# The order in which five engines take the stages of a fused macaron block, written out as explicit lists

## The chip, the cores and the metric

One core of a Trainium2 chip runs one program. The metric is the device time of that program in microseconds. The core has four compute engines, each with its own instruction stream: TensorE (PE in the profile), VectorE (DVE), ScalarE (ACT) and GpSimd (POOL); SyncE (SP) issues the DMAs. The streams run independently and meet only at semaphores.

## What is computed

The input x is 4 sequences of 1024 tokens with 128 features, all fp32. Three residual blocks follow each other:

```python
x = x + 0.5 * ffn(layernorm(x))
x = x + attn(layernorm(x))
x = x + 0.5 * ffn(layernorm(x))

def ffn(x):    # H = 512 hidden; m1, m2 are outer products of 16 tokens of the sequence
    h = x @ W1.T + scale * (x @ m1.T) + b1
    h = gelu(h, approximate=False)
    return h @ W2.T + scale * (h @ m2.T) + b2

def attn(x):   # 16 heads of 8; a linear attention over the whole sequence
    q, k, v = (split_heads(x @ W.T + b) for W, b in ((Wq, bq), (Wk, bk), (Wv, bv)))
    q, k = feature_map(q), feature_map(k)       # exp(x R - |x|^2 / 2), x over sqrt(8)
    kv = einsum('bhnd,bhne->bhde', k, v)
    z = 1 / (sum(q) + 1e-8)
    return merge(einsum('bhnd,bhde,bhn->bhne', q, kv, z)) @ Wo.T + bo
```

m1 and m2 depend on the sequence, so the FFN weights (W1 + scale m1) and (W2 + scale m2) are made anew for each sequence, in both FFN blocks.

## The kernel before

The 4096 tokens are cut into 8 chunks of 512, each held as 4 tiles of 128 tokens. A sequence is two chunks. FFN chunks are numbered 0 to 7 for the first FFN and 8 to 15 for the second, attention chunks 0 to 7. All activations stay in SBUF. Nothing is looped over on the chip: `build` writes each engine's stream, going through `plan(engine)`, a list of stages, and emitting for each one its waits and instructions.

A stage is written `name.chunk` or `name.chunk.part`, and may have halves on several engines. For an FFN chunk f:

- `stats.f`, `moments.f` (VectorE, L177, L189): mean and variance; `stats.f` on GpSimd (L196, L198): 1/sqrt by a power, giving `rstd`.
- `norm.f`: VectorE writes the normalised tiles `xn` (L546, four instructions); GpSimd then adds the bias to the whole chunk of X (L415).
- `turn.f`: TensorE transposes the four tiles into the bank `ps_t` (L690), ScalarE rounds to `xh` (L460), VectorE takes the rest `xl` (L565). The two halves of the number let the next matmuls keep precision.
- `up.f.j`, j = 0 to 3: three 512-wide matmuls (L718 to L720), then ScalarE's Gelu (L478). Two banks take turns, so `up.f.j` waits for the Gelu of two before it.
- `down.f.n`, n = 0 to 3: four fp32 matmuls, eight recorded instructions (L732); with n = 3, VectorE's residual add over the chunk (L614) and, for chunks 8 to 15, SyncE's store.

For a sequence i: `rows.i` writes 16 normalised tokens to DRAM and reads them back to every partition (`token_rows`, `ev`); `odd.i` (VectorE, L573) takes the other factor `od`; `w1.i` makes the weights of `up` on VectorE in twelve instructions, block by block (L590, L598, L602); `w2.i` makes those of `down` on GpSimd in two wide instructions, `w2m` and `w2e` (L425, L433). `up.2i.0` waits for the first block of `w1.i`, `down.2i.0` for `w2.i`. `od` and `ev` release both. `constants` and `split weights` prepare the attention weights once; `load` halves W2 on ScalarE.

For an attention chunk a: `astats`, `amoments`, `anorm`, `aturn` (as above, with the normalisation on ScalarE and GpSimd's add L419), `qk.a.n` (three matmuls, L749 to L751), `feat`, `head sums`, `exp` for the two halves of the chunk, `z sums`, `z eps`, `z` (VectorE, then GpSimd's product `qn`, L439), `qturn`, `gram`, per sequence `mix` in two parts, and `o.a` (TensorE L788, VectorE's add L659), after which the second FFN's `stats.(8+a)` may start. `turn.8` on TensorE waits for the add of `o.3`, since they share the bank `ps_t`.

The order of each engine's list comes from `TIMES`: for each engine, each of three phases and each stage, a time in steps of one chunk, for even and odd steps; `APART` overrides ten single stages. `plan` adds the step's number and sorts. No time of the table is waited for on the chip; it fixes only the order. Waits for buffers are in the stages themselves and do not depend on the order.

The lists that come out, in the stretches that the prediction speaks of (a blank in a name written as _):

```text
pool: stats.0 stats.1 norm.0 w2.0 stats.2 stats.3 norm.1 norm.2 w2.1
dve:  stats.0 moments.0 stats.1 moments.1 scale.0 norm.0 norm.1 odd.0 turn.0 w1.0 turn.1 stats.2 moments.2 stats.3 moments.3 norm.2 norm.3 odd.1 turn.2 constants.0 w1.1
pe:   warm_up.0.0 warm_up.0.1 turn.0 turn.1 up.0.0 up.0.1 up.0.2 up.0.3 up.1.0 up.1.1 down.0.0 up.1.2 up.1.3 turn.2 down.0.1 down.0.2 down.0.3 turn.3 down.1.0 down.1.1 split_weights.0 up.2.0
...
pool: stats.8 z.5 norm.8 anorm.7 stats.9 z.6 w2.4
dve:  o.2 feat.7.0 norm.8 z_sums.6 head_sums.7.1 o.3 z_eps.6 feat.7.1 z.6 mix.2.0 stats.9 odd.4 mix.2.1 turn.8 moments.9 w1.4 norm.9
pe:   o.3 turn.8 mix.2.0 gram.6 mix.2.1 qturn.5 o.4 gram.7 up.8.0 up.8.1 qturn.6 turn.9
...
pool: stats.15 w2.7 norm.15
dve:  norm.13 stats.14 down.10.3 turn.13 moments.14 norm.14 stats.15 odd.7 turn.14 moments.15 down.11.3 w1.7 norm.15
pe:   turn.14 up.13.2 up.13.3 down.12.2 down.12.3 down.13.0 down.13.1 up.14.0 up.14.1 turn.15
```

Of the kernel before, what the change touches and what calls it, by code (L numbers as in the profile page):

```python
# [27 lines left out]
SHIFT = 0.125  # L28
FC = 2 * CHUNKS

TIMES = {
    "sp": (
        {  # L40
# [21 lines left out]
        {
            "turn": (-0.62, -1.1), "up 0": (0.19, -0.18), "up 1": (0.33, -0.17), "load": (0.18, None),
            "up 2": (0.66, 0.39), "up 3": (0.81, 0.4), "split weights": (3.24, None), "anorm": (3.46, 3.85),
            "aturn": (4.84, 4.41),
        },
        {
            "feat 0": (0.34, 0.3), "feat 1": (0.96, 0.47), "exp 0": (1.35, 1.07), "exp 1": (1.42, 1.86),
            "gram": (None, 2.46), "qturn": (3.48, 4.43),
        },  # L70
        {
            "turn": (0.87, 0.49), "up 0": (1.44, 0.52), "up 1": (1.45, 0.53), "up 2": (1.5, 1.88),
            "up 3": (1.51, 1.89),
        },
    ),
    "dve": (
        {
            "stats": (-1.91, -2.53), "moments": (-1.9, -2.52), "norm": (-1.13, -2.1), "scale": (-1.14, None),
            "turn": (-0.39, -0.92), "odd": (-0.44, None), "w1": (-0.22, None), "constants": (1.62, None),
            "down 3": (2.12, 1.86), "astats": (2.49, 1.88), "amoments": (2.89, 3.11), "split weights": (3.57, None),  # L80
            "aturn": (4.91, 5.13),
        },
        {
            "head sums 0": (0.5, -0.02), "feat 0": (0.74, 0.67), "head sums 1": (0.95, 1.14),
            "feat 1": (0.97, 1.31), "z sums": (2.12, 1.92), "z eps": (2.28, 1.94), "z": (2.44, 1.96),
            "mix 0": (None, 3.51), "mix 1": (None, 3.93), "o": (4.99, 5.15),
        },
        {
            "stats": (-1.0, -0.48), "moments": (-0.97, -0.05), "norm": (-0.32, -0.02), "turn": (0.94, 0.02),
            "odd": (0.53, None), "w1": (0.97, None), "down 3": (3.01, 3.96),  # L90
        },
    ),
    "pe": (
        {
            "turn": (-0.89, -1.24), "warm up 0": (-1.13, None), "warm up 1": (-0.9, None), "up 0": (0.0, 0.0),
            "up 1": (0.14, 0.07), "up 2": (0.48, 0.09), "up 3": (0.55, 0.1), "down 0": (1.08, 0.8),
            "down 1": (1.12, 0.9), "down 2": (1.13, 1.29), "down 3": (1.66, 1.56), "split weights": (1.94, None),
            "aturn": (4.57, 4.14),
        },
        {  # L100
            "qk 0": (-0.22, 0.0), "qk 1": (-0.21, 0.01), "qk 2": (0.59, 0.16), "qk 3": (0.6, 0.17),
            "gram": (2.58, 2.15), "mix 0": (None, 2.8), "qturn": (3.18, 3.63), "mix 1": (None, 3.61),
            "o": (5.02, 4.23),
        },
        {
            "turn": (-0.63, 0.19), "up 0": (1.16, 0.25), "up 1": (1.17, 0.27), "up 2": (1.2, 0.81),
            "up 3": (1.22, 0.82), "down 0": (1.26, 1.64), "down 1": (1.28, 2.03), "down 2": (1.83, 2.21),
            "down 3": (2.62, 2.24),
        },
# [3 lines left out]
APART = {
    ("dve", "head sums", (2, 0)): 0.43,
    ("dve", "z sums", 7): 2.04,
    ("dve", "z eps", 1): 1.96,
    ("dve", "z eps", 7): 2.69,
    ("dve", "z", 1): 2.66,
    ("dve", "z", 7): 3.16,
    ("dve", "stats", 8): -2.28,  # L120
    ("dve", "moments", 8): -1.17,
    ("act", "anorm", 5): 3.35,
    ("act", "exp", (0, 0)): 0.76,
}


def work():

    for stage in ("load", "scale", "constants", "split weights"):
        yield stage, 0, 0, 0  # L130
    for k in range(2):
        yield "warm up", (0, k), 0, 0
    for f in range(FC):
        phase, step = (0, f) if f < CHUNKS else (2, f + CHUNKS)
        for stage in ("stats", "moments", "norm", "turn"):
            yield stage, f, phase, step
        if f % PER_B == 0:
            for stage in ("rows", "odd", "w1", "w2"):
                yield stage, f // PER_B, phase, step
        for j in range(HB):  # L140
            yield "up", (f, j), phase, step
        for n in range(NT):
            yield "down", (f, n), phase, step
    for a in range(CHUNKS):
        for stage in ("astats", "amoments", "anorm", "aturn"):
            yield stage, a, 0, a
        for n in range(NT):
            yield "qk", (a, n), 1, CHUNKS + a
        for p in range(2):
            yield "head sums", (a, p), 1, CHUNKS + a  # L150
            yield "feat", (a, p), 1, CHUNKS + a
            yield "exp", (a, p), 1, CHUNKS + a
        for stage in ("z sums", "z eps", "z", "gram", "qturn", "o"):
            yield stage, a, 1, CHUNKS + a
        if a % PER_B == PER_B - 1:
            for k in range(2):
                yield "mix", (a // PER_B, k), 1, CHUNKS + a
# [666 lines left out]
```

## Time and profile before

| | us |
|---|---|
| median of 3 runs | 191.21 |
| lowest, highest | 191.19, 191.68 |
| span of the profiled execution | 190.5 |
| TensorE busy | 172.3 |
| VectorE busy | 152.1 |
| ScalarE busy | 96.8 |
| GpSimd busy | 96.7 |
| mean granted TensorE clock | 0.981 |

The span runs from the first to the last instruction of one profiled execution. The page gives no other time for that execution; the median of the timed runs stands 0.7 us above its span. A busy TensorE is one with a matmul under way; two matmuls overlap a little, so their recorded lengths add up to more than the time they take. The chain of waits shows the time without the overlap. "issue" as a releaser means that the profile shows nothing that the engine waited for at that moment.

### The profile page before, as it was taken

Reading aid. Unit: us, or ns where it says so; the run is one execution under the profiler, and the core shown is the slowest. Engines: PE = TensorE matmul, PEld = TensorE weight load, DVE = VectorE, ACT = ScalarE, POOL = GpSimd, SP = SyncE. Lnnn points to the kernel's source line nnn. Section 1 sums busy time; section 2 is a strip of 40 time slices with the busy share of each in tenths; the row PEclk is TensorE's granted clock in tenths of the full one; section 3 lists DMA queues with packets and bytes.
Section 4 is the critical chain, followed back from the end, with each engine's and each line's share of the span. In section 5 each row is a group of like instructions: output and inputs, shape, how many; then the busy total and the mean of one; then the engine's idle time right before and its main releaser. Section 6 shows DMA issues by size and latency. Waiting matters only on the chain.

```text
span 190.5 us, 3499 instructions
## 1 busy us (share of the span) xinstructions
PE 172.3 (90%) x1115; PEld 150.9 (79%) x1115; DVE 152.1 (80%) x485; ACT 96.8 (51%) x170; POOL 96.7 (51%) x124
## 2 busy tenths in 40 slices
...
GB/s 139 222 135 252 109 6 0 3 109 3 5 110 5 0 0 0 3 2 0 0 3 0 0 2 112 0 3 44 69 0 58 112 57 55 34 137 23 87 3 110
DMA packets 17921, 9.60 MB, mean 50 GB/s; under 512 B 880, under 2 KB 17520, under 8 KB 17904
## 3 DMA queue, kind: packets, MB, share of 16 engines
...
q8 instruction: 9, 0.15, 0.3%
q14 instruction: 8, 0.07, 0.1%
...
## 4 chain that ended last, share of the span: by engine, by line
PE 55%; DVE 19%; issue 11%; DMA 7%; POOL 3%; ACT 2%; SPq 0%; DVEq 0%; POOLq 0%; ACTq 0%
PE quad L732 21%; PE quad L718 6%; DVE xn L546 6%; PE quad L720 5%; PE quad L719 5%; DMA ev<-token_rows 3%; PE ps_t L690 3%; PE quad L749 3%; DMA rows<-in_rows_dram 3%; PE quad L751 3%; PE quad L750 3%; DMA token_rows<-xn 1%; PE ps_g L767 1%; DVE ex L630 1%; DVE bst L177 1%
## 5 line engine op out<-in xcount | busy, mean ns | idle before, releaser
L478 ACT ACTIVATE gl<-quad,cols 128x512 f32<-128x512 f32 x64 | 43.5, 687 | 47.2 <-PE quad L720 46.4
L732 PEld LDWEIGHTS quad<-w2e,gl 128*128 128x128 f32 x496 | 60.8, 192 | 2.5
L732 PE MATMUL quad<-w2e,gl 128*128 128x128 f32 x496 | 62.0, 275 | 0.0
L546 DVE TENSOR_SCALAR xn<-X,mv,rstd 128x128 f32<-128x128 f32 x64 | 31.5, 555 | 6.2 <-POOL rstd L198 6.2
L718 PE MATMUL quad<-xh,w1h 128*128 128x512 f32 x64 | 29.4, 460 | 5.2 <-issue 4.0
L719 PE MATMUL quad<-xl,w1h 128*128 128x512 f32 x64 | 26.4, 413 | 0.0
L720 PE MATMUL quad<-xh,w1l 128*128 128x512 f32 x64 | 26.2, 410 | 0.0
L415 POOL TENSOR_TENSOR X<-X,b2h 128x512 f32<-128x512 f32 x16 | 20.4, 1281 | 8.7 <-DVE xn L546 8.7
L196 POOL TENSOR_SCALAR veps<-mv 128x4 f32<-128x4 f32 x16 | 4.3, 270 | 33.9 <-DVE mv L189 33.9
L614 DVE TENSOR_TENSOR X<-quad,X 128x512 f32<-128x512 f32 (+1 forms) x16 | 10.5, 658 | 13.6 <-PE quad L732 13.6
L718 PEld LDWEIGHTS quad<-xh,w1h 128*128 128x128 f32 x64 | 12.5, 196 | 8.9 <-issue 7.7
L460 ACT ACTIVATE xh<-ps_t 128x512 fp32r<-128x512 f32 x16 | 9.5, 592 | 19.2 <-PE ps_t L690 18.9
L198 POOL TENSOR_TENSOR rstd<-veps,mhalf 128x4 f32<-128x4 f32 x16 | 17.4, 1090 | 1.3
L690 PE MATMUL ps_t<-ident,xn 128*128 128x128 f32 x64 | 12.1, 289 | 5.6 <-DVE xn L546 2.9
L177 DVE BATCH_NORM_STATS2 bst<-X 128x6 f32<-128x128 f32 x64 | 13.7, 275 | 4.3 <-DMA X<-in_x_dram 4.3
L484 ACT ACTIVATE sq<-quad 128x512 f32<-128x512 f32 x16 | 9.5, 596 | 11.8 <-PE quad L751 11.6
L590 DVE SCALAR_TENSOR_TENSOR w1r<-ev,od,w1t 128x128 f32<-128x128 f32 x28 | 14.7, 544 | 1.0 <-issue 1.0
L690 PEld LDWEIGHTS ps_t<-ident,xn 128*128 128x128 f32 x64 | 7.8, 140 | 9.3 <-DVE xn L546 3.9
L720 PEld LDWEIGHTS quad<-xh,w1l 128*128 128x128 f32 x64 | 12.8, 200 | 3.0
L749 PE MATMUL quad<-wah,xah 128*128 128x512 f32 x32 | 13.9, 435 | 0.4 <-DVE ex L630 0.3
L468 ACT ACTIVATE xa<-X,anmr,arstd 128x128 f32<-128x128 f32 x32 | 13.1, 485 | 1.1 <-POOL anmr L409 1.1
L439 POOL TENSOR_TENSOR qn<-qk,zr 128x512 f32<-128x512 f32 x8 | 8.8, 1096 | 9.6 <-DVE zr L644 9.6
...
## 6 DMA issues: line engine op xcount, KB each, us to landing
ev<-token_rows SPq DMA_DIRECT2D x8, 512.0 KB, 3.8
...
```

The lines of the kernel that those rows point to most:

```text
L177: ins = dve.bn_stats(bst[:, i % 2, n], x[:, n])
L198: pool.tensor_tensor(rstd[:, i % 2], veps[:, i % 2], mhalf[:], ALU.pow).then_inc(s_rstd, 1)
L415: pool.tensor_tensor(X[:, xslot(i)], X[:, xslot(i)], b2h[:].unsqueeze(1).to_broadcast([P, NT, D]), ALU.add).then_inc(s_xb, 1)
L478: act.activation(gl[:, f % 2, j], ps_h[j % 2], ACT.Gelu, bias=cols[:, j:j + 1]).then_inc(s_gelu, 1)
L546: dve.tensor_scalar(xn[:, i % 2, n], X[:, xslot(i), n], mv[:, i % 2, n, 0:1], rstd[:, i % 2, n:n + 1], ALU.subtract, ALU.mult).then_inc(s_ ...
L590: dve.scalar_tensor_tensor(out=w1r[:, j], in0=even[:, j], scalar=od[:, j:j + 1], in1=w1t[:, j * D:(j + 1) * D], op0=ALU.mult, op1=ALU.add) ...
L690: ins = pe.transpose(ps_t[:, n * P:(n + 1) * P], xn[:, i % 2, n], ident[:])
L718: pe.matmul(ps_h[j % 2], w1h[:, w, blk], xh[:, f % 2], start=True, stop=False)
L719: pe.matmul(ps_h[j % 2], w1h[:, w, blk], xl[:, f % 2], start=False, stop=False)
L720: pe.matmul(ps_h[j % 2], w1l[:, w, blk], xh[:, f % 2], start=False, stop=True).then_inc(s_u, 1)
L732: ins = pe.matmul(y[:, n * P:(n + 1) * P], gl[:, f % 2, j, n * P:(n + 1) * P], w2e[:, f // PER_B % 2, j], start=(j == 0), stop=(j == HB - 1))
L749: pe.matmul(to, xah[:, a, tile], wah[:], start=True, stop=False)
```

## The change

`TIMES`, `APART` and `work` are removed. `ORDER` holds, for each engine, the list itself, and `plan` only splits it into words. Every stage of the lists before is in the lists after, once and on the same engine; the sequence differs on all five. What a stage emits, its waits, its buffers and its engine stay as they are. The new lists in full, with the removed tables cut:

```diff
@@ -28,145 +28,77 @@
 SHIFT = 0.125
 FC = 2 * CHUNKS
...
-TIMES = {
+ORDER = {
     "sp": (
-        {
-            "rows": (-0.84, None),
-        },
-        {
-        },
-        {
-            "rows": (-0.88, None), "down 3": (2.45, 2.43),
-        },
+        "rows.0 rows.1 rows.2 rows.3 rows.4 rows.5 rows.6 rows.7 down.8.3 down.9.3 down.10.3 down.11.3 down.12.3 "
+        "down.13.3 down.14.3 down.15.3 "
     ),
     "pool": (
-        {
-            "stats": (-2.74, -3.73), "norm": (-0.77, 0.15), "w2": (-0.75, None), "astats": (3.24, 2.28),
-            "anorm": (9.29, 8.79),
-        },
-        {
-            "z": (3.3, 2.34),
-        },
-        {
-            "stats": (-0.68, -1.2), "norm": (-0.65, 0.33), "w2": (1.31, None),
-        },
+        "stats.0 stats.1 stats.2 w2.0 norm.0 norm.1 stats.3 stats.4 w2.1 stats.5 stats.6 norm.2 w2.2 astats.0 stats.7 "
+        "astats.1 norm.3 norm.4 astats.2 norm.5 w2.3 astats.3 norm.6 norm.7 astats.4 astats.5 anorm.0 anorm.1 anorm.2 "
+        "astats.6 anorm.3 anorm.4 anorm.5 astats.7 z.0 z.1 z.2 z.3 z.4 anorm.6 stats.8 z.5 norm.8 stats.9 w2.4 "
+        "stats.10 stats.11 stats.12 z.6 w2.5 z.7 norm.9 norm.10 norm.11 stats.13 stats.14 anorm.7 w2.6 stats.15 "
+        "norm.12 norm.13 w2.7 norm.14 norm.15 "
     ),
     "act": (
...
+        "turn.0 up.0.0 load.0 turn.1 up.0.1 up.0.2 up.0.3 up.1.0 up.1.1 up.1.2 up.1.3 turn.2 turn.3 split_weights.0 "
+        "up.2.0 up.2.1 up.2.2 up.2.3 up.3.0 up.3.1 turn.4 up.3.2 up.3.3 turn.5 up.4.0 up.4.1 up.4.2 up.4.3 up.5.0 "
+        "anorm.0 turn.6 up.5.1 anorm.1 up.5.2 up.5.3 turn.7 up.6.0 up.6.1 up.6.2 aturn.0 anorm.2 aturn.1 up.6.3 "
+        "up.7.0 up.7.1 up.7.2 up.7.3 aturn.2 anorm.3 anorm.4 feat.0.0 anorm.5 exp.0.0 aturn.3 feat.0.1 feat.1.0 "
+        "aturn.4 exp.0.1 feat.1.1 feat.2.0 exp.1.0 exp.1.1 feat.2.1 anorm.6 feat.3.0 exp.2.0 exp.2.1 gram.1 aturn.5 "
+        "feat.3.1 anorm.7 aturn.6 exp.3.0 feat.4.0 exp.3.1 feat.4.1 aturn.7 qturn.0 feat.5.0 exp.4.0 exp.4.1 feat.5.1 "
+        "gram.3 qturn.1 feat.6.0 exp.5.0 exp.5.1 feat.6.1 qturn.2 qturn.3 feat.7.0 feat.7.1 exp.6.0 gram.5 exp.6.1 "
+        "exp.7.0 qturn.4 exp.7.1 turn.8 turn.9 qturn.5 up.8.0 up.8.1 gram.7 up.8.2 up.8.3 up.9.0 up.9.1 up.9.2 up.9.3 "
+        "turn.10 qturn.6 turn.11 up.10.0 up.10.1 turn.12 up.10.2 up.10.3 up.11.0 up.11.1 up.11.2 qturn.7 up.11.3 "
+        "up.12.0 up.12.1 turn.13 up.12.2 up.12.3 up.13.0 turn.14 up.13.1 up.13.2 up.13.3 up.14.0 up.14.1 turn.15 "
+        "up.14.2 up.14.3 up.15.0 up.15.1 up.15.2 up.15.3 "
     ),
     "dve": (
...
+        "stats.0 moments.0 stats.1 moments.1 scale.0 norm.0 odd.0 turn.0 norm.1 w1.0 stats.2 moments.2 turn.1 norm.2 "
+        "stats.3 stats.4 moments.3 constants.0 turn.2 moments.4 stats.5 down.0.3 odd.1 norm.3 norm.4 w1.1 astats.0 "
+        "turn.3 moments.5 stats.6 moments.6 turn.4 down.1.3 odd.2 norm.5 w1.2 norm.6 astats.1 amoments.0 down.2.3 "
+        "astats.2 stats.7 amoments.1 turn.5 moments.7 norm.7 turn.6 odd.3 w1.3 amoments.2 down.3.3 aturn.0 turn.7 "
+        "down.4.3 astats.3 astats.4 amoments.3 aturn.1 split_weights.0 down.5.3 amoments.4 astats.5 amoments.5 "
+        "down.6.3 aturn.2 astats.6 head_sums.0.0 amoments.6 feat.0.0 down.7.3 astats.7 aturn.3 head_sums.0.1 feat.0.1 "
+        "head_sums.1.0 feat.1.0 z_sums.0 amoments.7 head_sums.1.1 feat.1.1 head_sums.2.0 z_eps.0 feat.2.0 aturn.4 z.0 "
+        "head_sums.2.1 z_sums.1 feat.2.1 z_eps.1 head_sums.3.0 z.1 feat.3.0 aturn.5 z_sums.2 head_sums.3.1 z_eps.2 "
+        "feat.3.1 z.2 aturn.6 head_sums.4.0 z_sums.3 feat.4.0 head_sums.4.1 z_eps.3 aturn.7 feat.4.1 z.3 mix.0.0 "
+        "head_sums.5.0 mix.0.1 feat.5.0 z_sums.4 head_sums.5.1 z_eps.4 o.0 feat.5.1 stats.8 z.4 head_sums.6.0 mix.1.0 "
+        "moments.8 feat.6.0 o.1 z_sums.5 head_sums.6.1 mix.1.1 feat.6.1 z_eps.5 stats.9 z.5 norm.8 o.2 head_sums.7.0 "
+        "head_sums.7.1 moments.9 feat.7.0 o.3 feat.7.1 mix.2.0 norm.9 turn.8 odd.4 mix.2.1 w1.4 o.4 stats.10 turn.9 "
+        "o.5 moments.10 stats.11 stats.12 norm.10 moments.11 moments.12 z_sums.6 norm.11 z_eps.6 z.6 mix.3.0 z_sums.7 "
+        "stats.13 turn.10 odd.5 z_eps.7 w1.5 mix.3.1 moments.13 norm.12 turn.11 z.7 down.8.3 o.6 stats.14 moments.14 "
+        "down.9.3 odd.6 w1.6 turn.12 norm.13 norm.14 turn.13 o.7 down.10.3 stats.15 odd.7 moments.15 turn.14 w1.7 "
+        "norm.15 down.11.3 turn.15 down.12.3 down.13.3 down.14.3 down.15.3 "
     ),
     "pe": (
...
+        "warm_up.0.0 turn.0 warm_up.0.1 up.0.0 turn.1 up.0.1 up.0.2 up.0.3 up.1.0 up.1.1 up.1.2 turn.2 up.1.3 "
+        "down.0.0 down.0.1 down.0.2 down.0.3 down.1.0 split_weights.0 down.1.1 turn.3 down.1.2 down.1.3 up.2.0 up.2.1 "
+        "up.2.2 up.2.3 turn.4 up.3.0 up.3.1 down.2.0 up.3.2 down.2.1 up.3.3 down.2.2 down.2.3 turn.5 up.4.0 up.4.1 "
+        "down.3.0 up.4.2 down.3.1 down.3.2 up.4.3 down.3.3 up.5.0 turn.6 down.4.0 down.4.1 up.5.1 up.5.2 down.4.2 "
+        "down.4.3 up.5.3 turn.7 up.6.0 up.6.1 aturn.0 up.6.2 up.6.3 down.5.0 down.5.1 down.5.2 aturn.1 down.5.3 "
+        "up.7.0 up.7.1 aturn.2 up.7.2 up.7.3 down.6.0 down.6.1 qk.0.0 down.6.2 down.6.3 qk.0.1 down.7.0 down.7.1 "
+        "down.7.2 down.7.3 aturn.3 qk.0.2 qk.0.3 qk.1.0 qk.1.1 aturn.4 qk.1.2 qk.1.3 qk.2.0 qk.2.1 gram.0 qk.2.2 "
+        "qk.2.3 qk.3.0 qk.3.1 aturn.5 gram.1 qk.3.2 qk.3.3 gram.2 qk.4.0 aturn.6 qk.4.1 qturn.0 qk.4.2 qk.4.3 aturn.7 "
+        "gram.3 qk.5.0 qk.5.1 mix.0.0 qk.5.2 mix.0.1 qk.5.3 o.0 qk.6.0 qturn.1 qk.6.1 mix.1.0 qturn.2 qk.6.2 o.1 "
+        "qk.6.3 qk.7.0 mix.1.1 qk.7.1 qturn.3 o.2 qk.7.2 qk.7.3 gram.4 gram.5 o.3 qturn.4 mix.2.0 gram.6 turn.8 "
+        "mix.2.1 qturn.5 gram.7 turn.9 o.4 up.8.0 up.8.1 o.5 up.8.2 up.8.3 mix.3.0 up.9.0 up.9.1 down.8.0 up.9.2 "
+        "up.9.3 turn.10 down.8.1 down.8.2 down.8.3 down.9.0 mix.3.1 down.9.1 qturn.6 turn.11 up.10.0 up.10.1 down.9.2 "
+        "up.10.2 up.10.3 turn.12 o.6 down.9.3 up.11.0 up.11.1 qturn.7 up.11.2 up.11.3 down.10.0 down.10.1 down.10.2 "
+        "down.10.3 up.12.0 up.12.1 down.11.0 up.12.2 turn.13 down.11.1 down.11.2 o.7 down.11.3 up.12.3 up.13.0 "
+        "turn.14 up.13.1 up.13.2 down.12.0 down.12.1 down.12.2 down.12.3 up.13.3 up.14.0 turn.15 up.14.1 up.14.2 "
+        "down.13.0 down.13.1 down.13.2 up.14.3 down.13.3 up.15.0 up.15.1 down.14.0 up.15.2 up.15.3 down.14.1 "
+        "down.14.2 down.14.3 down.15.0 down.15.1 down.15.2 down.15.3 "
     ),
 }
...
 def plan(engine):
 
-    placed = []
-    for stage, i, phase, step in work():
-        name = f"{stage} {i[1]}" if isinstance(i, tuple) else stage
-        time = TIMES[engine][phase].get(name, (None, None))[step % 2]
-        if time is not None:
-            placed.append((step + APART.get((engine, stage, i), time), stage, i))
-    placed.sort(key=lambda p: p[0])
-    return [(stage, i) for _, stage, i in placed]
+    for word in ORDER[engine].split():
+        stage, *i = word.split(".")
+        i = tuple(int(k) for k in i)
+        yield stage.replace("_", " "), i if len(i) > 1 else i[0]
 
 
 def stats(dve, i, x, bst, s_bst, s_mv):
```

## Rows read from the trace of the kernel before

**Rows 1.** The page's busy table: us, share of the span, instructions.
```profile
PE 172.3 (90%) x1115; PEld 150.9 (79%) x1115; DVE 152.1 (80%) x485; ACT 96.8 (51%) x170; POOL 96.7 (51%) x124
```

**Rows 2.** Waits of TensorE: line, releaser, us in total, times, longest.
```profile
PE ps_t L690 <- DVE xn L546: 2.9, 4, 1.3
PE ps_r L672 <- DVE wb L525: 1.3, 1, 1.3
PE ps_m L706 <- DVE xal L576: 0.9, 1, 0.9
```

**Rows 3.** Windows: length; busy PE, PEld, DVE, ACT, POOL; granted clock; DMA.
```profile
10.00:15.00 5.00, 3.09 (x10) 2.24 (x11) 4.96 (x22) 1.80 (x3) 0.00 (x0) 0.76 0.59 174
78.00:114.00 36.00, 35.25 (x210) 29.63 (x208) 34.79 (x85) 24.15 (x50) 20.79 (x24) 1.00 0.00 1
120.00:125.00 5.00, 3.09 (x15) 1.96 (x15) 5.00 (x11) 2.14 (x4) 4.42 (x4) 1.00 0.00 0
125.00:130.00 5.00, 5.00 (x22) 4.35 (x23) 4.03 (x13) 2.13 (x4) 2.52 (x3) 0.66 0.01 3
```

**Rows 4.** The chain that ended last: start us, length us, what.
```profile
149.81 0.44 PE ps_t L690 x4
162.07 0.24 PE quad L718
162.77 0.89 PE quad L732 x8
```

**Rows 5.** Timeline: start, length in us, engine, line, operation, count, [wait before].
```profile
19.09 1.11 DVE L546 TENSOR_SCALAR xn<-X,mv,rstd 128x128 f32<-128x128 f32 x4 [1.88 <-POOL rstd L198]
19.35 1.04 POOL L198 TENSOR_TENSOR rstd<-veps,mhalf 128x4 f32<-128x4 f32 x1
20.36 2.52 POOL L415 TENSOR_TENSOR X<-X,b2h 128x512 f32<-128x512 f32 x2
20.42 3.05 DVE L546 TENSOR_SCALAR xn<-X,mv,rstd 128x128 f32<-128x128 f32 x4 [0.22 <-POOL rstd L198]
```

**Rows 6.** The timeline at 120 to 125 us.
```profile
120.70 1.21 POOL L439 TENSOR_TENSOR qn<-qk,zr 128x512 f32<-128x512 f32 x1
120.89 3.69 DVE L546 TENSOR_SCALAR xn<-X,mv,rstd 128x128 f32<-128x128 f32 x3
121.87 1.03 POOL L425 TENSOR_TENSOR w2m<-ev,od 128x512 f32<-128x512 f32 x1
122.98 1.52 POOL L433 TENSOR_TENSOR w2e<-w2m,w2t 128x512 f32<-128x512 f32 x1
```

**Rows 7.** Timeline of `w1.2` with `w2.2`, and of `w1.4` alone.
```profile
40.80 2.71 DVE L590 SCALAR_TENSOR_TENSOR w1r<-ev,od,w1t 128x128 f32<-128x128 f32 x2
41.83 1.53 POOL L433 TENSOR_TENSOR w2e<-w2m,w2t 128x512 f32<-128x512 f32 x1
44.35 0.47 PE L718 MATMUL quad<-xh,w1h 128*128 128x512 f32 x1 [0.97 <-issue]
...
118.52 0.57 DVE L590 SCALAR_TENSOR_TENSOR w1r<-ev,od,w1t 128x128 f32<-128x128 f32 x2
120.09 0.47 PE L718 MATMUL quad<-xh,w1h 128*128 128x512 f32 x1 [0.27 <-DVE w1l L602]
```

**Rows 8.** Timeline: TensorE's first instruction of `up.0.0` and of `up.2.0`.
```profile
12.56 0.69 PE L718 MATMUL quad<-xh,w1h 128*128 128x512 f32 x1 [0.68 <-DVE w1l L602]
...
29.24 0.47 PE L718 MATMUL quad<-xh,w1h 128*128 128x512 f32 x1
```

**Rows 9.** Timeline: `o.3` on VectorE, `up.12.0` and `up.14.0` on TensorE.
```profile
113.94 0.68 DVE L659 TENSOR_TENSOR X<-ps_t,X 128x512 f32<-128x512 f32 x1
...
156.41 0.47 PE L718 MATMUL quad<-xh,w1h 128*128 128x512 f32 x1 [1.19 <-issue]
...
172.20 0.47 PE L718 MATMUL quad<-xh,w1h 128*128 128x512 f32 x1 [1.54 <-issue]
```

**Rows 10.** DMA issues: count, KB each, median us from issue to landing.
```profile
ev<-token_rows SPq DMA_DIRECT2D x8, 512.0 KB, 3.8
```

88 lines of the change are left out of this document (removed).

## The prediction

> **What bounds the kernel now.** I read the busy table first: TensorE works 172.3 of 190.5 us, VectorE 152.1 [rows 1]. So the span is TensorE's work plus its stalls, and a new order can only change stalls. The waits of TensorE come next: it waits for VectorE's `xn` tiles, for `wb`, and for `w1l` [rows 2]. The windows show the third thing: from 78 to 114 us both engines are full (35.25 and 34.79 of 36 us), and twice the granted clock was low, at 10 to 15 us (0.76) and 125 to 130 us (0.66, so part of it at 1.2 instead of 2.4 GHz) [rows 3]. Last, the chain gives TensorE's step sizes: an `up` 0.70 us (162.07 to 162.77), a `down` 0.89, the four transposes of a chunk 0.44 [rows 4].
>
> The row that decides is one of VectorE beside GpSimd. A `norm` (four `xn` instructions) takes 1.11 us at 19.09, but 3.05 us at 20.42, where GpSimd runs two adds over a whole chunk (2.52 us) [rows 5]. At 120.89 it needs more than 3.69 us for three, beside `qn`, `w2m` and `w2e` [rows 6]: one `xn` gets through for each wide GpSimd instruction. The first block of `w1` is ready for TensorE 1.57 us after its start when GpSimd is quiet (118.52 to 120.09), and 3.55 us when `w2` lies beside it (40.80 to 44.35, with `w2e` ending at 43.36) [rows 7]. So what a new order is worth is which wide GpSimd work it puts beside which `norm` and `w1`. The diff adds no work; I followed it, adding these durations along the new lists.
>
> **Part 1, start to `up.2.0`.** Before, `up.0.0` starts at 12.56 and `up.2.0` at 29.24 [rows 8]. New: `norm.1` follows `turn.0` on VectorE, 1.1 us with GpSimd idle, so `w1.0` starts at 11.3 and `up.0.0` at about 12.8 (+0.2). `turn.1` now stands behind `up.0.0` on TensorE and behind `load.0` and a Gelu on ScalarE, so its VectorE half ends near 16.7. GpSimd has `stats.2` before `w2.0`: `rstd` is there at 16.3, and then `w2m`, `w2e` (1.03 and 1.53 us, [rows 6, 7]), `norm.0` and `norm.1` (1.26 us each, half of the 2.52 in [rows 5]) follow without a break until about 21.6. `norm.2` on VectorE starts at 16.65, right into these four, and ends near 21.8. TensorE's list has `turn.2` before `up.1.3` and before all of `down.0`, so it waits from 20.0 to 21.8, while `down.0` could have run from 19. VectorE goes on: `stats.3`, `stats.4`, `moments.3` (2.1), `constants` (about 2), `turn.2`, `moments.4`, `stats.5`, `down.0.3` to 28.3, then `odd.1`, which lets `w2.1` start beside `norm.3`: 31.6. `norm.4` 32.7, first block of `w1.1` 34.1. TensorE is idle from 29.3 to 31.6 before `turn.3` and 0.5 us before `up.2.0`. At 34.1 it has done two `down` more than before at 29.24 (1.8 us), so it is behind by 34.1 - 29.24 - 1.8 = 3.1 us. By idle time alone it is +2.4 (4.7 against 2.3) and +0.2 for the later start. I take 2.6.
>
> **Part 2, `up.2.0` to 80 us.** Of the old stalls (0.97 before `up.4.0` [rows 7], 0.9 for `xal` [rows 2], 0.3 before `up.6.0`) those for `xal` and `up.6.0` go: `aturn` now comes later. But ScalarE's `turn.4` stands behind `up.3.1`, so `norm.5` starts only at 42.1, again beside GpSimd's `norm.2` and `w2.2`, and TensorE loses 0.8 at `turn.5` and 1.2 at `up.4.0`. 2.0 against 2.3: -0.3. So at 80 us the new kernel is 2.3 us late.
>
> **Part 3, the full stretch.** The mark is the end of `o.3` on VectorE: 113.94 + 0.68 = 114.62 before [rows 9]. VectorE has no slack here, so what stands ahead of `o.3` in its list counts. Newly ahead: `aturn.4` 0.66, `stats.9` 0.85, `moments.9` 0.36; no longer: `z_sums.6` 0.65. That is +1.2. `norm.8` now stands right behind `z.5`, so GpSimd's `qn` (1.1 to 1.2 us, as in [rows 6]) lies on it: +1.0, of which I give back 0.6 for small VectorE gaps that close. Mark: 114.62 + 2.3 + 1.2 + 0.4 = 118.5.
>
> **Part 4, the mark to the end.** Before, 190.5 - 114.6 = 75.9 us. Three things get better. `norm.9` comes before `odd.4`, so `w2.4` can't lie beside it: 1.1 us instead of over 3.69 [rows 6], and TensorE has `turn.9` behind it early. `norm.12` and `norm.14` run long before `w1.6` and `w1.7` need their `ev` (its transfer takes 3.8 us [rows 10]), so the waits of 1.2 and 1.54 us before `up.12.0` and `up.14.0` [rows 9] go. Two get worse: `w1.4` and `w1.5` now lie beside `w2.4` and `w2.5`, 2 us each on the first block; and GpSimd's `norm.12` and `norm.13`, put behind `stats.15`, meet `w1.7` together with `w2.7`, which moves `norm.15` to 8 to 11 us behind TensorE's `turn.14`, where only 6.8 us of work cover it. Followed the stretch is 73.3 us with the last bunch at its lightest and 76.2 at its heaviest. I take 74.3, as the earlier steps of this part all gain.
>
> **The sum.** 118.5 + 74.3 = 192.8 us of span against 190.5. The median of the runs is 191.21, 0.7 above the span; so 193.5. Sizes I can't see: how much `xn` gets through before GpSimd takes over (+/-0.3 each time, some ten times), and a further low clock. Before, it was low after TensorE's waits ahead of `up.0.0` (the last 0.68 us [rows 8]), and again at 125 us after five microseconds in which TensorE worked 3.09 [rows 3]. New waits of 2.4 us before `up.8.0` can do the same; the old one is dropped with `turn.9`, so I count them even; at worst one more costs 1.7 us (three steps of 1.3 instead of 0.7).
>
> The Trainium skill, "SBUF — State Buffer", section "Who interferes with whom", says that the loser of the port shared by VectorE and GpSimd is blocked for the whole of the other's instruction. The rows on wide operands agree. By its letter the narrow GpSimd instructions would block too; but the trace has the narrow power (1.04 us at 19.35) beside `norm.2` (1.11 us for four, as fast as alone) [rows 5]. So they cost nothing in my sum; by the rule they would cost up to 1.04 us at `norm.7` (beside `astats.1`) and at `norm.11` (beside `stats.12`), 2 us in all, and the estimate would be 195.6.
>
> **Rivals.** (a) *Slower, as summed*: 192.3 to 194.9, chance 0.45. (b) *Faster*: the bunches are lighter than I have them. The one mechanism: `norm.2` gets most of its four `xn` through before `w2m` locks, and so `norm.3` and `norm.5`. Then `turn.2` is there at 18, TensorE loses nothing in part 1 and 2 (0 to +0.3), the mark is at 115.5, and with 73.3 to 74 behind it the span is 188.8 to 189.5: 189.5 to 190.3 measured. For it: VectorE's totals are the same and part 4 loses real waits; against it: the one-by-one pattern in [rows 5, 6]. It decides where `norm.2` ends before 19.5. Chance 0.30. (c) *No change*, 190.6 to 191.8: part 1 is late by 2 but VectorE's slack after 60 us swallows it before the mark. Against it: TensorE is full from 61 to 80 us in both. 0.10. (d) *Clearly slower*, 195 to 197: the heaviest bunch at `w1.7` (76.2) and one more stretch at 1.2 GHz: 118.5 + 76.2 + 1.7 + 0.7 = 197.1. 0.13, and 0.02 more for blocked narrow instructions. That the change does nothing is excluded: the lists have the same 219, 195, 142, 64 and 16 entries, but the order differs on every engine.
>
> **Numbers.** A measurement tells 0.3%, 0.57 us, from no change. Faster is (b), 0.31 with a little of (c); the same 0.09; slower 0.60. The range takes in most of (b) and of (d): 189.3 to 196.5.
>
> **What would show it.** `norm.2` on VectorE over 4 us long and an idle TensorE before `turn.2`, `turn.3`; `up.2.0` at 33 to 35 us; the end of `o.3` at 117 to 119; `up.12.0` without a wait; `norm.15` later than 8 us behind `turn.14`. It is wrong if `norm.2` takes less than 3 us, or if `up.2.0` starts before 32.

## The result: 193.6 us against 191.2, and a profile that does not show it

| | before | after |
|---|---|---|
| median of the first runs, us | 191.20 (4 runs) | 193.58 (4 runs) |
| lowest, highest | 191.18, 191.68 | 191.95, 194.15 |
| span of the profiled execution | 190.5 | 190.2 |
| its mean granted clock | 0.981 | 0.982 |

The ratio is 1.013, with a 95% interval of 1.0071 to 1.0189. Twelve more runs of the changed kernel (first experiment) gave 193.36, ratio 1.0071 (1.0034 to 1.0108). So the change costs 0.7 to 1.3% by the two estimates, a small loss but one clear of both intervals. Medians are of all executions; the ratios leave out those that took over 1.5% more than the fastest of the same kernel.

The two profiled executions differ by 0.3 us, the wrong way round. The profiled one of after was the fastest of its four: an execution's time is its span and 1.7 us, so 191.95 is 190.2, and the median of 193.4 over all sixteen executions is a span near 191.65. The spans of the other three were 191.3, 192.4 and 192.4, at granted clocks of 0.973, 0.965 and 0.965. What the change costs has to be looked for in the clock as well as in the trace.

The page after, busy table, answers to [rows 1]:

```profile
PE 170.8 (90%) x1115; PEld 149.5 (79%) x1115; DVE 149.2 (78%) x485; ACT 96.1 (51%) x170; POOL 96.3 (51%) x124
```

VectorE is busy 2.9 us less with the same 485 instructions: fewer of them are held up by GpSimd. Yet TensorE's waits for `xn` and `w1l` are longer than before (line, releaser, us in total, times, longest; L622, L650 and L478 are the L690, L718 and L546 of before, since the tables above them are shorter):

```profile
PE ps_t L622 <- DVE xn L478: 7.1, 5, 3.7
PE quad L650 <- DVE w1l L534: 4.4, 2, 2.3
PE quad L650 <- issue: 2.7, 3, 1.6
```

[rows 2] has the 2.9 us for `xn` of before; two further lines of the same view of before are needed beside it:

```profile
PE quad L718 <- issue: 4.0, 4, 1.5
PE quad L718 <- DVE w1l L602: 0.9, 2, 0.7
```

2.9 us for `xn` have become 7.1, one of these waits 3.7 us long, and 0.9 us for `w1l` have become 4.4. Against that, the waits under "issue" fell from 4.0 to 2.7, and those for `wb` and `xal` are gone. On balance TensorE is without a matmul for 19.4 us (190.2 less 170.8) instead of 18.2 (190.5 less 172.3): little is lost in sum, but more of it in single long waits. The windows say where, and what follows; they answer to [rows 3] (length, busy PE, PEld, DVE, ACT, POOL, clock, DMA, GB/s):

```profile
78.00:114.00 36.00, 35.67 (x213) 30.04 (x212) 35.20 (x83) 24.40 (x50) 18.07 (x22) 1.00 0.02 6
120.00:125.00 5.00, 2.82 (x15) 2.24 (x16) 5.00 (x18) 2.94 (x5) 1.03 (x1) 1.00 0.00 0
165.00:170.00 5.00, 1.33 (x7) 0.83 (x5) 5.00 (x8) 1.38 (x2) 4.13 (x4) 0.95 0.00 0
170.00:175.00 5.00, 5.00 (x27) 4.32 (x27) 2.27 (x5) 1.80 (x3) 1.28 (x1) 0.70 0.19 52
```

From 165 to 170 us TensorE works 1.33 of 5 us, while VectorE is full and GpSimd nearly so. Then the granted clock is 0.70: part of the next window runs at 1.2 GHz. Before, that happened at 125 to 130 us [rows 3].

The stretch in the middle of it, on VectorE (start, length, engine, line, operation, tiles):

```profile
162.78 1.36 DVE L522 SCALAR_TENSOR_TENSOR w1r<-ev,od,w1t 128x128 f32<-128x128 f32 x1
164.06 1.30 DVE L530 CAST w1h<-w1r 128x128 fp32r<-128x128 f32 x1
165.28 1.14 DVE L534 TENSOR_TENSOR w1l<-w1r,w1h 128x128 fp32r<-128x128 f32 x1
166.48 2.87 DVE L534 TENSOR_TENSOR w1l<-w1r,w1h 128x128 fp32r<-128x128 f32 x2
169.28 1.10 DVE L478 TENSOR_SCALAR xn<-X,mv,rstd 128x128 f32<-128x128 f32 x4
```

on GpSimd at the same time:

```profile
162.51 2.77 POOL L347 TENSOR_TENSOR X<-X,b2h 128x512 f32<-128x512 f32 x2
165.23 1.04 POOL L357 TENSOR_TENSOR w2m<-ev,od 128x512 f32<-128x512 f32 x1
166.35 1.58 POOL L365 TENSOR_TENSOR w2e<-w2m,w2t 128x512 f32<-128x512 f32 x1
167.90 1.31 POOL L347 TENSOR_TENSOR X<-X,b2h 128x512 f32<-128x512 f32 x1
```

and on TensorE:

```profile
169.76 1.15 PE L622 MATMUL ps_t<-ident,xn 128*128 128x128 f32 x4 [3.67 <-DVE xn L478]
```

Five wide GpSimd instructions in a row (162.5 to 169.2 us), and beside each about one of VectorE's twelve gets through. `w1.7` lasts 7.8 us, from 161.5 to 169.35, where a `w1` with GpSimd quiet takes 2.5 (experiment 6). `norm.15` stands behind it, `turn.15` behind that.

### The profile page after: what moved, and what is told of

It is laid out like the page before. It is cut to its first block, busy times and chain, and to the rows that moved or that the text cites. A ratio compares the mean times of both kernels' runs of the same rounds, so it can differ in the third digit from the quotient of the medians.

```text
span 190.2 us, 3499 instructions
## 1 busy us (share of the span) xinstructions
PE 170.8 (90%) x1115; PEld 149.5 (79%) x1115; DVE 149.2 (78%) x485; ACT 96.1 (51%) x170; POOL 96.3 (51%) x124
## 4 chain that ended last, share of the span: by engine, by line
PE 63%; DVE 21%; issue 8%; ACT 3%; DMA 3%; SPq 0%; DVEq 0%
PE quad L664 23%; DVE xn L478 8%; PE quad L650 7%; PE quad L651 6%; PE quad L652 6%; PE quad L681 3%; PE ps_t L622 3%; DVE w1r L522 3%; PE quad L683 3%; PE quad L682 3%; DMA rows<-in_rows_dram 3%; PE ps_g L699 2%; DVE w1l L534 2%; PE ps_m L638 2%; DVE bst L109 1%
## 5 line engine op out<-in xcount | busy, mean ns | idle before, releaser
L664 PEld LDWEIGHTS quad<-w2e,gl 128*128 128x128 f32 x496 | 59.5, 192 | 2.0
L664 PE MATMUL quad<-w2e,gl 128*128 128x128 f32 x496 | 60.2, 275 | 0.0
L650 PE MATMUL quad<-xh,w1h 128*128 128x512 f32 x64 | 29.3, 458 | 7.6 <-DVE w1l L534 4.4
L478 DVE TENSOR_SCALAR xn<-X,mv,rstd 128x128 f32<-128x128 f32 x64 | 29.4, 523 | 2.3 <-POOL rstd L130 2.3
L650 PEld LDWEIGHTS quad<-xh,w1h 128*128 128x128 f32 x64 | 12.7, 198 | 12.3 <-issue 10.5
L128 POOL TENSOR_SCALAR veps<-mv 128x4 f32<-128x4 f32 x16 | 4.5, 282 | 34.1 <-DVE mv L121 34.0
L546 DVE TENSOR_TENSOR X<-quad,X 128x512 f32<-128x512 f32 (+1 forms) x16 | 10.5, 658 | 11.6 <-PE quad L664 11.6
L622 PE MATMUL ps_t<-ident,xn 128*128 128x128 f32 x64 | 12.1, 301 | 7.2 <-DVE xn L478 7.1
L130 POOL TENSOR_TENSOR rstd<-veps,mhalf 128x4 f32<-128x4 f32 x16 | 16.9, 1053 | 1.3
L622 PEld LDWEIGHTS ps_t<-ident,xn 128*128 128x128 f32 x64 | 8.5, 148 | 10.9 <-issue 4.5
L497 DVE TENSOR_TENSOR xl<-ps_t,xh 128x512 fp32r<-128x512 f32 x16 | 10.9, 680 | 7.5 <-ACT xh L392 7.5
L522 DVE SCALAR_TENSOR_TENSOR w1r<-ev,od,w1t 128x128 f32<-128x128 f32 x28 | 15.4, 571 | 0.5 <-DVE od L505 0.5
L681 PE MATMUL quad<-wah,xah 128*128 128x512 f32 x32 | 14.4, 450 | 0.3 <-DVE ex L562 0.3
```

The lines of the kernel that those rows point to most:

```text
L130: pool.tensor_tensor(rstd[:, i % 2], veps[:, i % 2], mhalf[:], ALU.pow).then_inc(s_rstd, 1)
L478: dve.tensor_scalar(xn[:, i % 2, n], X[:, xslot(i), n], mv[:, i % 2, n, 0:1], rstd[:, i % 2, n:n + 1], ALU.subtract, ALU.mult).then_inc(s_ ...
L522: dve.scalar_tensor_tensor(out=w1r[:, j], in0=even[:, j], scalar=od[:, j:j + 1], in1=w1t[:, j * D:(j + 1) * D], op0=ALU.mult, op1=ALU.add) ...
L622: ins = pe.transpose(ps_t[:, n * P:(n + 1) * P], xn[:, i % 2, n], ident[:])
L650: pe.matmul(ps_h[j % 2], w1h[:, w, blk], xh[:, f % 2], start=True, stop=False)
L664: ins = pe.matmul(y[:, n * P:(n + 1) * P], gl[:, f % 2, j, n * P:(n + 1) * P], w2e[:, f // PER_B % 2, j], start=(j == 0), stop=(j == HB - 1))
```

## Experiments

Each had 6 to 12 runs, beside 11 to 35 of the kernel before in the same job. Times are medians. "The changed kernel" without a number stands for the 193.36 us of the first experiment. Experiments 1 to 4, 5 to 8, and 9 and 10 ran together, with medians of the kernel before of 191.83, 191.80 and 191.39 us.

**1. The changed kernel once more.** No edit.

> The changed kernel as it is, for more executions beside the kernel before. Its four times so far lie between 191.95 and 194.15 us, with granted clocks from 0.982 down to 0.965. Clock theory: the time follows the granted clock, in steps of about 1.1 us for each further stretch at 1.2 GHz, and no execution is under 191.9. Wait theory (the prediction's sum): the time is lost in waits that are there in every execution, so the spread is chance and not tied to the clock. Both expect a median of 193 to 194.

Measured: 193.36 us, 191.83 to 195.18. With a clock for every execution, the spans sort like this (the kernel before from all jobs, the changed kernel from both of its):

| mean granted clock | before: executions, median span | after: executions, median span |
|---|---|---|
| 0.989 to 1.0 | 46, 189.8 | 0 |
| 0.981 to 0.982 | 16, 190.15 | 5, 190.5 |
| 0.973 | 7, 191.7 | 8, 191.5 |
| 0.965 | 0 | 3, 192.4 |

At the same clock the two orders take the same time, within 0.35 us in the medians. These are small groups with a wide spread: the five of the new order at 0.982 lie between 190.1 and 192.0 us, so the mean clock does not fix the time. What differs clearly is how often they get which clock: two thirds of the old order's executions run at 0.989 or better, none of the sixteen of the new one. The medians of the clock groups lie 1.0 and 0.9 us apart, near the 1.1 of the clock theory; the fastest execution, 191.83, is just under its 191.9. The windows of the profiled execution of this run, beside those above:

```profile
165.00:170.00 5.00, 1.38 (x6) 0.77 (x5) 5.00 (x7) 1.38 (x2) 4.42 (x4) 0.90 0.00 0
170.00:175.00 5.00, 4.95 (x17) 4.24 (x18) 2.54 (x6) 1.86 (x3) 1.28 (x1) 0.50 0.17 52
```

The same wait, but here the whole of 170 to 175 us runs at 1.2 GHz: 17 matmuls instead of 27. Its span is 191.7 against 190.2.

**2. Work in the waits.** Idle matmuls on TensorE ahead of `up.8.0`, `up.10.0` and `turn.15`.

```diff
 if stage == "turn":
...
+    for n in range(FILL_TURN.get(i, 0)):        # {15: 14}
+        pe.matmul(ps_t[:, 0:P], ident[:], ident[:], start=True, stop=True)
...
 if stage == "up":
...
+    if j == 0 and f in FILL:                    # {8: 10, 10: 6}
+        wait(pe, s_gelu, HB * f - 1)
+        for n in range(FILL[f]):
+            pe.matmul(quad[:, 0, 0:P], ident[:], ident[:], start=True, stop=True)
     pe.wait_ge(s_w1, LORA * (f // PER_B) + j + 1)
```

> The changed kernel, with idle matmuls on TensorE (identity by identity, results overwritten) inside three of its long waits: 10 ahead of up.8.0, 6 ahead of up.10.0, 14 ahead of turn.15. They do nothing for the result and end before the wait would. Clock theory: the extra low-clock stretches vanish, every execution has a clock of 0.98 or more, the median falls to 191.5 to 192.2 and the spread below 0.5 us. Wait theory: nothing is gained, 193 to 194.

Measured: 191.02 us, ratio 0.9952 (0.9917 to 0.9986); 190.47 to 192.01, but for one execution of the twelve that was disturbed throughout (251.4 us at a clock of 0.66). Ten of the other eleven had a clock of 0.989 or more, eight of them 0.991 with a median span of 189.2. On TensorE (timeline):

```profile
165.92 3.29 PE L625 MATMUL ps_t<-ident 128*128 128x128 f32 x28
169.69 1.10 PE L628 MATMUL ps_t<-ident,xn 128*128 128x128 f32 x4 [0.47 <-DVE xn L482]
```

and the windows:

```profile
165.00:170.00 5.00, 4.53 (x35) 4.04 (x33) 5.00 (x8) 1.38 (x2) 4.15 (x4) 1.00 0.01 3
170.00:175.00 5.00, 5.00 (x36) 4.48 (x36) 2.29 (x5) 1.75 (x3) 1.31 (x1) 1.00 0.18 54
```

`turn.15` starts at 169.69, where it started at 169.76: this wait was filled, not shortened. But the clock stays at 2.4 GHz, and 36 matmuls run from 170 to 175 us. 2.3 us for work that computes nothing: the low clock was a cost of its own, and the wait theory's 193 to 194 falls. The gain is larger than the clock theory had it (191.5 to 192.2), and the eleven undisturbed executions spread over 1.5 us instead of its 0.5. The old order was never filled, so it is not known what it would gain by the same.

**3 and 4. Half the lists each.** The lists are cut at the moment at which `o.3` ends on VectorE in the changed kernel.

```diff
-ORDER = new lists
+ORDER = {e: [s for s in old[e] if s in first[e]] + [s for s in new[e] if s not in first[e]] for e in new}   # 3
+ORDER = {e: [s for s in new[e] if s in first[e]] + [s for s in old[e] if s not in first[e]] for e in new}   # 4
```

> The old order for all stages that start before VectorE's o.3 ends (115.7 us in the changed kernel), the new order for the rest. Prediction's sum: part 1 and 2 cost 2.3 us, so without them 191.2. Clock theory: the three long waits of TensorE all lie behind the mark, so this stays scattered and slow, 192.3 to 194.

> The new order up to the same mark, the old order for the rest. Prediction's sum: it keeps the late start, 193.5. Clock theory and the profile after (mark at 115.7 against 114.6, with 1.2 us of VectorE work moved ahead of it): close to the kernel before, 190.5 to 191.8, with little spread.

Measured: old then new 193.57 us, ratio 1.0105 (1.0068 to 1.0142), within the clock theory's range; new then old 192.11 us, ratio 1.0015 (0.9983 to 1.0047), 0.3 above it. The sum of the prediction had 191.2 and 193.5, so it put the loss into the wrong half. The second half of the new lists carries the whole loss, the first half none that can be measured. With the cut, the third kernel's `o.3` ends 2.3 us earlier than the changed kernel's (113.74 against 116.05 in the profile of experiment 1), but `up.8.0` starts at 122.6 and 122.5: stages that the old order had put off (VectorE's `stats.9` and `moments.9` among them) stand between. So the cut shows which half costs, not what the first half would be worth with a better second.

The third kernel also limits what the clock explains. Nine of its twelve executions had a mean clock of 0.981 or 0.982, with a median span of 191.8, where the old order has 190.15 at the same clock. So its loss of 1.7 us is there at an equal mean clock: it lies in waits.

**5. The bunch at `w1.7` taken apart.** One edit in GpSimd's list.

```diff
-"stats.10 stats.11 stats.12 z.6 w2.5 z.7 norm.9 norm.10 norm.11 stats.13 stats.14 anorm.7 w2.6 stats.15 "
-"norm.12 norm.13 w2.7 norm.14 norm.15 "
+"stats.10 stats.11 stats.12 z.6 w2.5 z.7 norm.9 norm.10 norm.11 stats.13 stats.14 anorm.7 w2.6 norm.12 "
+"norm.13 stats.15 w2.7 norm.14 norm.15 "
```

> The changed kernel with one edit: on GpSimd norm.12 and norm.13 stand ahead of stats.15 instead of behind it. In the changed kernel they run at 162.5 to 165.3 us, beside w1.7, which takes 7.8 us, and TensorE waits 3.67 us for turn.15. Collision theory: w1.7 falls to 4.5 to 5 us, turn.15 waits 0.5 to 1.2, no low clock follows it, and the median falls from 193.4 by 2.5 to 4 us, to 189.5 to 191. Rival, that norm.15 is late for another reason (its rstd or w2.7): w1.7 shorter but the time within 0.7 us of 193.4.

Measured: 190.09 us, ratio 0.9911 (0.9878 to 0.9943): 3.3 us less than the changed kernel. TensorE's wait:

```profile
167.38 1.01 PE L624 MATMUL ps_t<-ident,xn 128*128 128x128 f32 x4 [1.50 <-DVE xn L480]
```

3.67 us have become 1.50. `w1.7` takes 5.7 us, more than I expected, since `w2.7` and the add of `norm.14` still lie on it. That no low clock would follow was wrong too:

```profile
165.00:170.00 5.00, 3.50 (x14) 2.41 (x13) 3.60 (x9) 2.24 (x4) 2.78 (x3) 0.90 0.08 25
170.00:175.00 5.00, 5.00 (x32) 4.77 (x32) 1.29 (x2) 1.19 (x3) 0.00 (x0) 0.76 0.28 80
```

So most of the 3.3 us is the wait itself. At equal mean clocks this kernel's median span is 2.2 us (at 0.973, four executions against eight) and 2.5 us (at 0.981 and 0.982, six against five) below the changed kernel's, and the wait became 2.2 us shorter. Two instructions moved on an engine that is busy half of the time turn the change from slower to faster than before.

**6. `w2` kept off `w1`.** One wait on GpSimd, for sequences 4 and 5.

```diff
 if stage == "w2":
     pool.wait_ge(s_ev, 16 * (i + 1))
     pool.wait_ge(s_od, i + 1)
+    if i in (4, 5):
+        pool.wait_ge(s_w1, LORA * (i + 1))
```

> The changed kernel with one added wait: GpSimd's w2.4 and w2.5 start only when w1.4 and w1.5 are finished on VectorE. Collision theory: w1.4 falls from 4.7 to 2.5 us and w1.5 likewise, TensorE's waits of 2.3 us at up.8.0 and 1.55 us at up.10.0 nearly go, nothing waits for the later w2, and the median falls by 2.5 to 4 us, to 189.5 to 191. Rival, that the time comes back at turn.15: 192.5 to 193.5.

Measured: 189.70 us, ratio 0.9889 (0.9857 to 0.992). `w2m` now starts at 122.05, after `w1.4`, which takes 2.5 us (119.34 to 121.82) instead of 4.7:

```profile
119.34 0.61 DVE L526 SCALAR_TENSOR_TENSOR w1r<-ev,od,w1t 128x128 f32<-128x128 f32 x2
...
121.33 0.49 DVE L538 TENSOR_TENSOR w1l<-w1r,w1h 128x128 fp32r<-128x128 f32 x2
```

In the changed kernel the same first row is

```profile
118.38 2.81 DVE L522 SCALAR_TENSOR_TENSOR w1r<-ev,od,w1t 128x128 f32<-128x128 f32 x2
```

`up.8.0` starts 1.6 us after `w1.4` does instead of 3.8, as in [rows 7], and TensorE has no wait for the later `w2`. An added wait made the kernel 3.7 us faster, although the 3.7 us wait at `turn.15` and the low clock around it (0.79 from 165 to 170 us) are still there.

**7. The start.** GpSimd's `norm.0` and `norm.1` ahead of `stats.2`.

```diff
-"stats.0 stats.1 stats.2 w2.0 norm.0 norm.1 stats.3 stats.4 w2.1 stats.5 stats.6 norm.2 w2.2 astats.0 stats.7 "
+"stats.0 stats.1 norm.0 norm.1 stats.2 w2.0 stats.3 stats.4 w2.1 stats.5 stats.6 norm.2 w2.2 astats.0 stats.7 "
```

> The changed kernel with one edit at the start: GpSimd's norm.0 and norm.1 stand ahead of stats.2, where GpSimd is idle, instead of beside VectorE's norm.2. Collision theory: norm.2 falls from 5.0 to 2.7 to 3.0 us (w2.0 still lies on it), up.2.0 moves from 32.8 to 30.7, and all that follows moves with it: 191 to 192. Rival, that VectorE's full stretch swallows it: up.2.0 2 us earlier, the end of o.3 less than 0.7 us earlier, and the time within 0.7 us of 193.4.

Measured: 192.34 us, 1.0 less than the changed kernel, with one of twelve executions disturbed (203.15 us at a clock of 0.837); ratio to before 1.0035 (1.0006 to 1.0063). That interval overlaps the changed kernel's, so the gain itself is uncertain. `norm.2` is as short as expected, but VectorE then waits:

```profile
17.56 2.93 DVE L480 TENSOR_SCALAR xn<-X,mv,rstd 128x128 f32<-128x128 f32 x4
...
24.75 0.69 DVE L499 TENSOR_TENSOR xl<-ps_t,xh 128x512 fp32r<-128x512 f32 x1 [0.67 <-ACT xh L394]
...
27.18 0.69 DVE L548 TENSOR_TENSOR X<-quad,X 128x512 f32<-128x512 f32 x1 [0.70 <-PE quad L666]
```

2.0 us gained at `norm.2`, 1.4 of it given back at `turn.2` and `down.0.3`. And the edit makes a collision of its own, since GpSimd was idle but VectorE was not: the add of `norm.1` now lies beside `w1.0`.

```profile
11.49 1.26 POOL L349 TENSOR_TENSOR X<-X,b2h 128x512 f32<-128x512 f32 x1 [1.57 <-DVE xn L480]
11.84 1.00 DVE L532 CAST w1h<-w1r 128x128 fp32r<-128x128 f32 x1
13.57 0.77 PE L652 MATMUL quad<-xh,w1h 128*128 128x512 f32 x1 [1.77 <-DVE w1l L536]
```

The cast takes 1.00 us where it took 0.22, and `up.0.0` starts 2.25 us after `w1.0` instead of 1.48 (at 13.57, where the changed kernel has 12.49). From `up.0.0` to `up.2.0` it is 19.9 us against 20.3, so `up.2.0` starts at 33.45, 0.7 us later than in the changed kernel. Neither expectation is met in full: the gain is swallowed before `up.2.0`, and not in the full stretch. Where the measured 1.0 us comes from stays open; the profiled execution had a clock of 0.963, low from 10 to 19 us, too low to compare by.

**8. The known collisions apart.** Edits 5 and 7, the wait of 6 for sequences 1 to 7, and GpSimd's `norm.2` right behind `w2.0`.

```diff
-"stats.0 stats.1 stats.2 w2.0 norm.0 norm.1 stats.3 stats.4 w2.1 stats.5 stats.6 norm.2 w2.2 astats.0 stats.7 "
+"stats.0 stats.1 norm.0 norm.1 stats.2 w2.0 norm.2 stats.3 stats.4 w2.1 stats.5 stats.6 w2.2 astats.0 stats.7 "
...
+    if i in (1, 2, 3, 4, 5, 6, 7):
+        pool.wait_ge(s_w1, LORA * (i + 1))
```

> The changed kernel with all collisions that I know of taken apart: the two edits before, GpSimd's norm.2 right behind w2.0, and w2.1 to w2.7 each waiting until w1 of the same sequence is finished. TensorE's, VectorE's and ScalarE's lists are the changed ones. Collision theory: the single gains add up, 7 to 9 us, 184.5 to 187, under both kernels. Rival, that another chain ends last once these are gone: 187 to 190.

Measured: 182.82 us, ratio 0.9511 (0.9474 to 0.9548). That is 10.5 us under the changed kernel, more than the 7 to 9 that I expected. The edits were made together, so it is not known what each adds here. Its busy table:

```profile
PE 166.4 (92%) x1115; PEld 146.8 (81%) x1115; DVE 144.5 (80%) x485; ACT 95.7 (53%) x170; POOL 95.8 (53%) x124
```

VectorE is busy 144.5 us instead of 149.2 with the same instructions, and the low stretch of the clock behind `turn.15` is gone (mean clock 1.0 in this execution, 0.981 to 1.0 over six). Not all collisions are gone. The cast in `w1.0` still takes 0.99 us beside the add of `norm.1`, `norm.12` takes 3.10 us beside `w2.5`, `norm.13` and `norm.14` meet five wide GpSimd instructions, and `norm.15` meets `w2.7`:

```profile
143.48 7.14 DVE L482 TENSOR_SCALAR xn<-X,mv,rstd 128x128 f32<-128x128 f32 x8
...
157.60 4.37 DVE L482 TENSOR_SCALAR xn<-X,mv,rstd 128x128 f32<-128x128 f32 x4
```

**9. The waits with the old order.**

```diff
-ORDER = new lists
+ORDER = old lists
...
+    if i in (1, 2, 3, 4, 5, 6, 7):
+        pool.wait_ge(s_w1, LORA * (i + 1))
```

> The old order on all five engines, with one added wait: w2.1 to w2.7 on GpSimd each start only when w1 of the same sequence is finished. Question: is the gain of the version with all collisions apart one of the waits alone, or of the new order with the waits. Waits alone: w1.2, w1.3, w1.6 and w1.7 fall from 4.5 to 2.5 us, the stalls at up.4.0, up.12.0 and up.14.0 go, but norm.9 and norm.13 still meet w2: 188 to 189.5 us. Order and waits together: the old order stays above 188, since norm.9 costs 4 us in it whatever the waits, and the new order was 182.8. Rival, that the order is without any merit of its own: 184 or less.

Measured: 188.30 us, ratio 0.9847 (0.98 to 0.9894), inside what I expected. `norm.9` still takes 4 us beside `qn` and `w2.4`:

```profile
115.95 3.95 DVE L482 TENSOR_SCALAR xn<-X,mv,rstd 128x128 f32<-128x128 f32 x4
```

So the waits are worth about 3 us to the old order. The new order with them and the five moved adds (`norm.0`, `norm.1`, `norm.2`, `norm.12`, `norm.13`) is 5.5 us better still. This pair does not split those 5.5 us between the order and the moved adds, since the old order was not given the adds.

**10. `w2.7` kept off `norm.15` too.**

```diff
     if i in (1, 2, 3, 4, 5, 6, 7):
         pool.wait_ge(s_w1, LORA * (i + 1))
+    if i == 7:
+        pool.wait_ge(s_xn, NT * FC)
```

> The version with all collisions apart (182.8 us), with one more wait: w2.7 also waits for the last xn tile of norm.15, which it now stretches to 4.4 us. Collision theory: norm.15 1.1 us, the waits inside turn.15 go, 1.5 to 2.5 us less: 180.5 to 181.5. Rival, that down.14 then waits for w2.7: no change, 182.3 to 183.3.

Measured: 181.85 us, ratio 0.9496 (0.9452 to 0.954), the best of all; 1.0 us under the eighth, less than the 1.5 to 2.5 of the expectation. Its `norm.15`:

```profile
158.31 1.11 DVE L484 TENSOR_SCALAR xn<-X,mv,rstd 128x128 f32<-128x128 f32 x4
```

The ranges of the two overlap (180.93 to 182.81 and 181.66 to 184.85), so the size of this last step is only roughly known. The other stretched stages of experiment 8 are still there.

## Why the prediction came out right, and where its steps did not

The time (193.5 against 193.58) and the sign are right, and that collisions of GpSimd with VectorE cost time is shown by experiments 5, 6 and 8. But that the sum comes within 0.1 us is luck: its errors cancel. Step by step, against the profiled execution after:

| step | predicted | measured |
|---|---|---|
| `up.0.0` starts | 12.8 | 12.5 |
| `norm.2` on VectorE | 16.65 to 21.8 | 16.44 to 21.40 |
| `up.2.0` starts | 34.1 | 32.8 |
| late at 80 us | 2.3 | 0.9 |
| `o.3` ends (the mark) | 118.5 | 115.7 |
| mark to end | 74.3 | 74.5 |
| outside the span | 0.7 | 1.7 |
| median execution over the profiled | 0 | 1.4 |

**Part 1.** The row that the argument stood on:

```profile
16.44 4.96 DVE L478 TENSOR_SCALAR xn<-X,mv,rstd 128x128 f32<-128x128 f32 x4
...
21.45 0.33 PE L622 MATMUL ps_t<-ident,xn 128*128 128x128 f32 x1 [0.66 <-DVE xn L478]
...
30.20 0.59 PE L622 MATMUL ps_t<-ident,xn 128*128 128x128 f32 x2 [1.16 <-DVE xn L478]
```

`norm.2` is stretched to 4.96 us as written, and both waits of TensorE are there. Their sizes are not: I had it idle 2.3 us at `turn.3`, and it was 1.2, since `odd.1` came at 27.1 instead of 28.4. Stage lengths that I rounded up made 1.3 us by `up.2.0`: 1.8 us late instead of the 2.6 that I took.

**Part 2.** The waits for `xal` and at `up.6.0` went, and `turn.4` kept VectorE idle (2.6 us before 39.3), both as said. The step gained 0.9 us, not 0.3: at 78 us TensorE is 0.43 us later and has one `aturn` (0.44 us) less behind it, 0.9 in all. `up.4.0` waited 0.97 us.

**Part 3, the mark, is the step that failed.** It put the mark at 118.5 and not at 115.7. Of these 2.8 us parts 1 and 2 made half (2.3 us late by 80 us, measured 0.9); the other half arose here. From `head sums.0.1` to the mark VectorE took 34.6 us before and 35.25 after, +0.65 where I had +1.6. `norm.8` beside `qn` cost 0.7 (1.84 against 1.11 us), near the 1.0. What I missed is on GpSimd: six of the `anorm` adds, all of which had run beside VectorE's full stretch (85 to 101 us), now run at 75 to 84.5 us. Before, three of them had held up the product `qn`, which at 88.93 us then met `z eps.1` (0.86 us); now `z eps.1` meets nothing and takes 0.18. That is 0.7 of the 0.95 us that I had too much; I had followed VectorE's list there and not GpSimd's. Experiments 3 and 4 say the same in another way: I charged 3.9 us to the lists ahead of the mark and credited 1.6 behind it, and measured the first half as even (1.0015) and the second as the loss (1.0105).

**Part 4.** Nearly every piece is there: `norm.9` 1.10 us, `up.12.0` without a wait, 2.29 us before `up.8.0`, 1.55 before `up.10.0`, `norm.15` ending 10.7 us behind `turn.14`. The stretch took 74.5 us. But this is for the fastest of the first four executions, with a clock of 0.70 behind `turn.15`, where the profile of experiment 1 has 0.50.

**The clock is the term that I mis-sized.** I wrote that the old low stretch goes with `turn.9`, a new one may come, "so I count them even". It is not even: the new order never reached 0.989, the old one did in two of three executions, and filling three waits brings 2.3 us back. By the medians of the first experiment's table that is nearly the whole of the difference between the two kernels; what weakens this is that the table's groups are small and that the third kernel loses 1.7 us at an equal clock. The 0.7 us outside the span was wrong too. The executions with both numbers have 1.7 to 1.9, but for one that was disturbed; by that, the profiled execution of before took about 192.2 us, 1 us above the median that I compared it with. Against the 193.5 of the sum: mark -2.8, part 4 +0.2, offset +1.0, clock +1.4 make 193.3; the median over all sixteen executions is 193.36.

**The rule on the shared port.** The trace after repeats the case: `norm.7` beside a narrow power on GpSimd,

```profile
53.19 1.11 DVE L478 TENSOR_SCALAR xn<-X,mv,rstd 128x128 f32<-128x128 f32 x4 [1.54 <-POOL rstd L130]
```

```profile
53.45 1.04 POOL L130 TENSOR_TENSOR arstd<-aveps,mhalf 128x4 f32<-128x4 f32 x1
```

Neither is longer than alone, so my leaving narrow instructions out was right. The Trainium skill, "SBUF — State Buffer", section "Who interferes with whom", has the loser blocked for the other's whole instruction: with wide operands the trace agrees (one `xn` or one step of `w1` for each GpSimd instruction), with 128x4 it does not.

**The rivals.** (b), that `norm.2` slips through, is excluded by its 4.96 us. (c), that slack swallows the late start, has some truth: at the mark the new kernel was 1.1 us late, no more than the 1.2 us of work that stands newly ahead of it. (d), the heaviest bunch at `w1.7` with a further stretch at 1.2 GHz, is what happened in kind (7.8 us, and the clock), only on an earlier mark.
